# Pair products for one layer of a recommendation tower: four selected features per row instead of one per product tile, and another way of pacing the gathers

## The chip, the core and the metric

The kernel runs on one core of a Trainium2 chip. The metric is the device time of one launch in microseconds (us). A profiled execution gives the span (first to last instruction), and the engines are named as the profile does: PE (TensorE, with PEld for its weight loads), DVE (VectorE), ACT (ScalarE), POOL (GpSimd), SP (SyncE, which issues the ordinary DMAs).

## The reference

512 rows of input each carry 39 ids. Each id picks 16 numbers from its own table, so a row becomes 39 features of 16 numbers (`D`). Then:

```python
# X0, Xi: [b, 39, 16]
z  = einsum('bmd,bnd->bdmn', X0, X0)      # all products of two features
Xi = einsum('bdp,po->bod', z, W0)         # layer 1: 39*39 products -> 128
z  = einsum('bmd,bnd->bdmn', X0, Xi)      # 39 features by 128 outputs
X2 = einsum('bdp,po->bod', z, W1)         # layer 2 -> 128
h  = concat([sum over d of Xi, sum over d of X2, dense_ctx])
y  = relu(relu(h @ W_top1 + b1) @ W_top2 + b2) @ W_top3
```

The product of features n and m is the same as that of m and n, so layer 1 needs 39*40/2 = 780 products, with the two weights added.

## The kernel before

**Tiles, chunks, steps.** The 512 rows are 4 tiles of 128 (`TILES`). A tile is 4 chunks of 32 rows; a chunk is 32*16 = 512 columns (`CH`). Products are laid out over partitions: 780 of them are 7 product tiles (`PT`), six of 128 partitions and a last one with the remaining few, which stand there three times (for a high, a low and a second high part). One product tile of one chunk is one step `s`; 16 chunks times 7 are 112 steps (`STEPS`), 28 a tile (`SPT`). All engines run through the same list of steps in order, each with its own part of the work, and meet at semaphores.

**A step.** PE selects one factor for each of the 128 partitions with a matmul against a 0/1 matrix (`select`, 117 rows, because each feature is held as three bf16 parts) into one of two PSUM banks `b_bank`. DVE multiplies it by the other factor (`multiply`). That other factor, `xa`, is selected once a chunk (`fill_a`) and copied to SBUF by ACT (`take_a`). ACT rounds the product to the matmul's reduced type (`round_z`), DVE subtracts to get the remainder (`rest_z`), and PE, 5 steps later (`LAG`), adds weight times product into `l1_bank` in three matmuls: high by high, high by low, low by high (`layer1`). `l1_used` counts these steps. In tile 0 two product tiles of each seven are "direct": the product goes unrounded into one fp32 matmul, with no rounding and no remainder. `selected`, `product`, `rounded` and `remainder` are the semaphores between these parts.

**The rest of a chunk.** When its 7 steps are through, ACT copies the layer-1 result (`take_xi`, L545, at step 7i+11 of chunk i), PE turns it (`turn_xi`), and both it and the turned `xa` (`turn_a`) are split into high and low parts. SP spreads the latter into a block-diagonal matrix `diag` with 8 DMAs a chunk, and `g_block` multiplies the two in 4 blocks. ACT copies each block (`take_g`). `layer2` of a whole tile follows over the next tile's steps, 78 instructions a tile, from step 45 (`S2_AT`). After the last step come the last tile's layer 2 and the end of the top network.

**The features of a tile.** Those of small tables come from a matrix lookup at the start. Those of large tables come from POOL: one indirect DMA (a gather, L355) per table and tile, 98 in all: 20 for tile 0, 20 for tile 1, 29 for tile 2, 29 for tile 3, in this order. From tile 1 on, a fill of a scratch tile and a wait on it stand before each gather. In three groups of columns, features are then split into bf16 parts by ACT and DVE (`keep_top`, `rest_hi` and so on) at steps `SPLIT_AT` of the tile before; they wait for the gathers of their group (`gathered`). PE turns the parts at `X_AT` and ACT copies them into `xs`.

```python
nc.gpsimd.memset(pad[:], 0.0).then_inc(rested, 1)      # POOL, L353
pool.wait_ge(rested, fills_done)
nc.gpsimd.indirect_dma_start(feat[...], None, tables[order[n]], ...)
```

Of the kernel before, what the change touches and what calls it, by code (L numbers as in the profile page):

```python
# [16 lines left out]

# [15 lines left out]
PT = -(-PAIRS // P)  # L33
REST = PAIRS - (PT - 1) * P
REST_AT = (0, F, 2 * F)
REST_LO = 64
REST_ROWS = 96
ROWS = [P] * (PT - 1) + [REST_ROWS]
assert REST <= F and REST_AT[1] >= 32 and REST_AT[1] + REST <= REST_LO <= REST_AT[2] and REST_AT[2] + REST <= REST_ROWS
# [11 lines left out]
DIRECT = [[1, 4], [], [], []]  # L51
WHOLE = 2
Z_LAG = 2
Z_RING = Z_LAG + 2
LEAD = 1
RING = LAG + 2
LOOK_P = 125
# [8 lines left out]
REST_COLS = 192  # L66
FREE_FIRST = 8
W1_PIECES = 3
# [27 lines left out]
def direct(s):  # L96

    return s % PT in DIRECT[s // (CPT * PT)]


SPLITS = [sum(not direct(q) for q in range(s)) for s in range(STEPS)]
DIRECT_STEPS = [s for s in range(STEPS) if direct(s)]
# [8 lines left out]
def build(nc, ids, row_numbers, small_tables, tables, order, dense_t, w0_pair, w0_mirror, w1,  # L111
# [30 lines left out]
    with ctx:  # L142
# [19 lines left out]
        xa = sb("xa", [P, 2, P, D])  # L162
        sel = sb("sel", [R, PT + 1, P], bf16)
        id16 = sb("id16", [P, P], bf16)
        id32 = sb("id32", [P, P])
        z = sb("z", [P, Z_RING, CH])
# [6 lines left out]
        w0_rest = sb("w0_rest", [REST_ROWS, O], f32r)  # L173
# [49 lines left out]
        for (lo, hi), c in zip(classes, class_blocks):  # L223
# [50 lines left out]
        rested = sem("rested")  # L274
# [5 lines left out]
        chunk0_taken = sem("chunk0_taken")  # L280
        xt_hi_done = sem("xt_hi_done")
# [48 lines left out]

        def after(sems, *job):

            k, n = fill[job]
            return sems[k], n + 1
# [5 lines left out]
        def _(pool):  # L340

            pool.wait_ge(ids_in, 16)
            sent, fills_done = 0, 0
# [65 lines left out]
        def _(act):  # L409
# [111 lines left out]
            def round_z(s):  # L521
                rows = ROWS[s % PT]
                if direct(s):
                    return
# [290 lines left out]
        def _(pe):  # L815
# [286 lines left out]
            mlp3(1)  # L1102


def _pairs():

# [93 lines left out]
```

## Time and profile before

| | us |
|---|---|
| median of 3 runs (263.24 to 263.35) | 263.35 |
| the profiled execution's own time | 262.94 |
| its span | 260.9 |
| PE busy | 235.9 (90%) |
| DVE busy | 196.1 (75%) |
| ACT busy | 168.6 (65%) |
| POOL busy | 128.8 (49%) |

Busy time is a union over the instructions of an engine. The ends of matmuls are modelled, so a stretch in which PE is busy throughout means that it was never seen idle, not that every column of its array worked. Starts of instructions on PE are of more use than durations.

### The profile page before, as it was taken

How to read it: one execution, taken by the hardware profiler on the slowest of the kernel's cores; microseconds unless marked ns; L12 is line 12 of the kernel's file. 1: busy time of each engine (PE TensorE's matmuls, PEld its weight loads, DVE VectorE, ACT ScalarE, POOL GpSimd, SP SyncE). 2: the span in 40 equal slices, each digit the busy share in tenths (PEclk: the TensorE clock that was granted, in tenths of full speed). 3: DMA queues.
4: the chain of work that ended last, by engine and by line, in shares of the span. 5: the costliest groups of instructions: out<-in, count | busy, mean ns of one | idle time of the engine just before them, and what ended most of it. 6: DMA issues, size and time to landing. Idle time of an engine off the chain costs nothing.

```text
span 260.9 us, 5243 instructions
## 1 busy us (share of the span) xinstructions
PE 235.9 (90%) x1848; PEld 182.4 (70%) x1848; DVE 196.1 (75%) x341; ACT 168.6 (65%) x324; POOL 128.8 (49%) x180
## 2 busy tenths in 40 slices
PE   4998856989799978939999999999999999999996
PEld 4997733555466754737777777777787888898795
DVE  1799969998879999556889999879989877624001
ACT  4997555675787886547759878686757655466203
POOL 4788888888888888878888882000000000000000
PEclk9999755899999999988999999999999999999999
DMA  5920001545026540200221111010110101010000
GB/s 160 233 45 10 9 5 13 112 83 129 8 27 147 122 96 7 28 8 9 45 33 20 24 11 28 5 25 7 21 16 12 25 1 25 4 25 0 3 0 0
DMA packets 30883, 10.30 MB, mean 39 GB/s; under 512 B 21018, under 2 KB 30138, under 8 KB 30858
## 3 DMA queue, kind: packets, MB, share of 16 engines
q1 hardware_dynamic: 27722, 9.17, 16.3%
q0 software_dynamic: 3136, 0.81, 3.5%
q8 instruction: 14, 0.23, 0.4%
q14 instruction: 11, 0.09, 0.1%
HBM read 7.34 MB, written 0.00 MB: 28 GB/s over the span
## 4 chain that ended last, share of the span: by engine, by line
PE 48%; POOL 26%; DVE 12%; issue 9%; ACT 3%; DMA 2%; DVEq 0%; ACTq 0%
POOL feat L355 21%; PE s_bank L964 11%; POOL pad L353 5%; PE b_bank L904 4%; PE l_bank L925 4%; PE l_bank L927 4%; PE l_bank L926 4%; DVE z L716 3%; DVE w_sb L660 3%; DVE z_lo L730 3%; PE g_bank L949 2%; PE g_bank L950 2%; PE g_bank L951 2%; PE xi_bank L934 1%; ACT g L448 1%
## 5 line engine op out<-in xcount | busy, mean ns | idle before, releaser
L355 POOL DMA_INDIRECT feat<-tbl,ids_sb x98 | 107.3, 1095 | 29.4 <-POOL pad L353 21.1
L716 DVE TENSOR_TENSOR z<-xa,b_bank 128x512 f32<-128x512 f32 (+1 forms) x112 | 76.1, 684 | 17.3 <-PE b_bank L904 13.8
L529 ACT ACTIVATE z_hi<-z 128x512 fp32r<-128x512 f32 (+1 forms) x104 | 65.6, 630 | 18.9 <-DVE z L716 17.5
L730 DVE TENSOR_TENSOR z_lo<-z,z_hi 128x512 fp32r<-128x512 f32 x88 | 60.3, 686 | 0.0
L904 PE MATMUL b_bank<-xs,sel 117*128 117x512 bf16 (+1 forms) x112 | 45.2, 406 | 8.7 <-DVE z L716 8.6
L964 PE MATMUL s_bank<-g,w_sb 128*128 128x128 f32 x312 | 46.3, 278 | 0.0
L964 PEld LDWEIGHTS s_bank<-g,w_sb 128*128 128x128 f32 x312 | 42.2, 192 | 1.3 <-issue 0.7
L925 PE MATMUL l_bank<-z_hi,w_hi 128*128 128x512 f32 x88 | 41.8, 474 | 0.0
L904 PEld LDWEIGHTS b_bank<-xs,sel 117*128 117x128 bf16 (+1 forms) x112 | 11.5, 103 | 38.3 <-DVE z L716 20.7
L537 ACT ACTIVATE g<-g_bank 128x320 f32<-128x320 f32 x64 | 27.7, 432 | 16.3 <-PE g_bank L951 16.0
L927 PE MATMUL l_bank<-z_hi,w_lo 128*128 128x512 f32 x88 | 35.1, 399 | 0.0
L926 PE MATMUL l_bank<-z_lo,w_hi 128*128 128x512 f32 x88 | 35.0, 398 | 0.0
L949 PE MATMUL g_bank<-diag,xit_hi 128*128 128x320 f32 x64 | 29.5, 462 | 3.2 <-ACT g L537 3.2
L353 POOL MEMSET pad<- 128x192 f32 x78 | 21.3, 273 | 0.1
L950 PE MATMUL g_bank<-diag,xit_hi 128*128 128x320 f32 x64 | 20.1, 313 | 0.0
L951 PE MATMUL g_bank<-diag,xit_lo 128*128 128x320 f32 x64 | 19.9, 310 | 0.0
L927 PEld LDWEIGHTS l_bank<-z_hi,w_lo 128*128 128x128 f32 x88 | 16.8, 191 | 3.8
L949 PEld LDWEIGHTS g_bank<-diag,xit_hi 128*128 128x128 f32 x64 | 12.6, 197 | 8.1 <-issue 5.9
L925 PEld LDWEIGHTS l_bank<-z_hi,w_hi 128*128 128x128 f32 x88 | 17.1, 194 | 1.3 <-issue 0.8
L926 PEld LDWEIGHTS l_bank<-z_lo,w_hi 128*128 128x128 f32 x88 | 17.1, 194 | 0.2
L545 ACT ACTIVATE xi<-l_bank 128x512 f32<-128x512 f32 x16 | 9.6, 597 | 9.0 <-PE l_bank L922 9.0
L560 ACT ACTIVATE g<-b_bank,bt_sb 128x384 f32<-128x384 f32 (+1 forms) x8 | 3.7, 473 | 15.8 <-PE b_bank L1005 11.0
(190 smaller groups left out, 368.2 us busy)
## 6 DMA issues: line engine op xcount, KB each, us to landing
diag<-xt SPq DMA_DIRECT2D x128, 20.0 KB
w_sb<-w SPq DMA_DIRECT2D x3, 832.0 KB
feat<-tbl,ids_sb POOLq DMA_INDIRECT x98, 2.4
wt_sb<-wt SPq DMA_DIRECT2D x2, 512.0 KB, 4.7
g<-small SPq DMA_DIRECT2D x1, 770.0 KB
g<-small SPq DMA_DIRECT2D x1, 448.0 KB
w0p<-w_pair SPq DMA_DIRECT2D x1, 448.0 KB
w0m<-w_mirror SPq DMA_DIRECT2D x1, 448.0 KB
```

Source lines behind the costliest of these rows:

```text
L353: nc.gpsimd.memset(pad[:], 0.0).then_inc(rested, 1)
L355: nc.gpsimd.indirect_dma_start(feat[:, bt % 2, n * D:(n + 1) * D], None, tables[order[n]], bass.IndirectOffsetOnAxis(ids_sb[:, bt, order[n ...
L529: nc.scalar.activation(z_hi[0:rows, s % RING, :], z[0:rows, at, :], ACT.Copy).then_inc(rounded, 1)
L537: nc.scalar.activation(g[:, bt % 2, :, block * SB:(block + 1) * SB], g_bank[:, 0:SB * GW].rearrange("p (b m) -> p m b", m=GW), ACT.Copy).t ...
L716: nc.vector.tensor_tensor(target, xa[0:rows, bt % 2, c * CB:(c + 1) * CB, :].rearrange("p b d -> p (b d)"), b_bank[s % B_RING][0:rows, :], ...
L730: nc.vector.tensor_sub(low[first:rows, s % RING, :], z[first:rows, SPLITS[s] % Z_RING, :], z_hi[first:rows, s % RING, :].bitcast(f32)).the ...
L904: nc.tensor.matmul(b_bank[s % B_RING][0:ROWS[t], :], sel[:, t, 0:ROWS[t]], columns(bt, c), start=True, stop=True).then_inc(selected, 1)
L925: nc.tensor.matmul(bank[:], w0_hi[:, t, :], z_hi[:, slot, :], start=t == 0, stop=False)
L926: nc.tensor.matmul(bank[:], w0_hi[:, t, :], z_lo[:, slot, :], start=False, stop=False)
L927: nc.tensor.matmul(bank[:], w0_lo[:, t, :], z_hi[:, slot, :], start=False, stop=False).then_inc(l1_used, 1)
L949: nc.tensor.matmul(o, y_hi, x_hi, start=True, stop=False)
L964: last = nc.tensor.matmul(s2_bank[:, 0:P], w1_sb[:, order[m], :], g[:, bt % 2, m, :], start=m == 0, stop=m == F - 1)
```

## The change

It does four things.

- **Selection.** Each partition holds four features, chosen so that the six products of two of them (`PRODUCTS`) fill six product tiles. The first factor is selected as before (`fill_a`). Selections 0, 1 and 3 give the other three, selection 2 gives what the last product tile (`REST_T`) multiplies with the first factor. So a chunk has 4 calls of `select` instead of 7. ACT copies selections 0 and 1 to SBUF (`take_factor`); on chunk 0 DVE copies the second of them. `factors` holds three factors of two chunks.
- **Groups.** `multiply`, `round_z` and `rest_z` go by four groups of a chunk: 2 product tiles, 1 (the last tile, 128 rows now, of which 34 get a remainder), 3 and 1. A group is one instruction. `layer1` keeps its 7 steps and its matmuls. A group's buffers are taken again one chunk later. In tile 0 only the last group is direct (one product tile of seven instead of two).
- **Gathers.** The fills are gone. Each gather from the 31st on waits until one more step of layer 1 is done.
- **Times.** The splits, turns and first selections of tiles 2 and 3 stand some steps later in the list; `split_w0` comes before the copy of `xs` on DVE.

```diff
-REST_ROWS = 96
+FACTORS = 4
+PRODUCTS = ((0, 1), (0, 2), (3, 0), (3, 1), (3, 2), (1, 2))
+REST_LO = slice(64, 98)
+T_OF = (0, 1, REST_T, 2, 3, 4, 5)
+GROUPS = ((0, 2, 0, 0), (2, 1, REST_T, 2), (3, 3, 2, 3), (6, 1, 5, 2))
+REST_AT_STEP = {2: 0, 4: 1, 6: 2, 8: 3}
+SELECTS = 4
-DIRECT = [[1, 4], [], [], []]
+DIRECT_CHUNKS = 4
-Z_RING = Z_LAG + 2
+Z_SLOTS = 6
+PACED_FROM = 30
-SPLIT_AT = [[], [8, 14, 19], [8, 14, 19], [9, 16, 21]]
-X_AT = [[], [21, 22], [21, 22], [23, 24]]
-A_AT = [0, 24, 24, 26]
+SPLIT_AT = [[], [8, 14, 19], [9, 16, 23], [9, 16, 23]]
+X_AT = [[], [21, 22], [25, 26], [25, 26]]
+A_AT = [0, 24, 27, 27]
+SELECT_AT = [-4, -2, -1, 0]
+TILE_SELECT_AT = [None, [-4, -2, -1, 0], [0, 0, 1, 2], [0, 0, 1, 2]]
...
-                        if bt:
-                            fills_done += 1
-                            nc.gpsimd.memset(pad[:], 0.0).then_inc(rested, 1)
-                            pool.wait_ge(rested, fills_done)
+                        if bt and sent >= PACED_FROM:
+                            pool.wait_ge(l1_used, sent - PACED_FROM + 1)
...
+            def take_factor(i, k):
+                act.wait_ge(selected, SELECTS * i + k + 1)
+                if i >= 2:
+                    act.wait_ge(product, NG * (i - 1))
+                nc.scalar.activation(factors[:, i % 2, 1 + k, :], b_bank[k][:], ACT.Copy).then_inc(factor_taken, 1)
...
+            def round_z(i, k):
+                if direct(i, k):
                     return
-                act.wait_ge(product, s + 1)
-                if s >= RING:
-                    act.wait_ge(l1_used, s - RING + 1)
-                nc.scalar.activation(z_hi[0:rows, s % RING, :], z[0:rows, at, :], ACT.Copy).then_inc(rounded, 1)
+                first, count, slot, at = GROUPS[k]
+                act.wait_ge(product, NG * i + k + 1)
+                if i:
+                    act.wait_ge(l1_used, (i - 1) * PT + first + count)
+                nc.scalar.activation(z_hi[:, slot:slot + count, :], z[:, at:at + count, :],
+                                     ACT.Copy).then_inc(rounded, 1)
...
+            def multiply(i, k):
+                if k == 0:
+                    ...
+                    target = z[:, 0:2, :]
+                    one = factors[:, i % 2, 0, :].unsqueeze(1).broadcast_to([P, 2, CH])
+                    other = factors[:, i % 2, 1:3, :]
+                elif k == 1:
+                    ...
+                    target, one, other = z[:, 2, :], factors[:, i % 2, 0, :], b_bank[0][:]
+                elif k == 2:
+                    ...
+                    target = z[:, 3:6, :]
+                    one = factors[:, i % 2, :, :]
+                    other = b_bank[1][:].unsqueeze(1).broadcast_to([P, 3, CH])
                 else:
+                    ...
+                    one, other = factors[:, i % 2, 1, :], factors[:, i % 2, 2, :]
+                nc.vector.tensor_tensor(target, one, other, ALU.mult).then_inc(product, 1)
...
+            def select(i, q):
+                if q == 0:
                     features_there(i)
+                if q < 2:
+                    if i:
+                        pe.wait_ge(product, NG * (i - 1) + 2 + q)
+                else:
+                    pe.wait_ge(*taken_factor(i, q - 2))
+                nc.tensor.matmul(b_bank[q % B_RING][:], sel[:, q, :], columns(*divmod(i, CPT)),
                                  start=True, stop=True).then_inc(selected, 1)
```

## Rows read from the trace of the kernel before

**Rows 1.** The page: 40 equal slices of the span, busy tenths and clock.
```profile
PE   4998856989799978939999999999999999999996
PEclk9999755899999999988999999999999999999999
```

**Rows 2.** Windows between copies of a chunk's layer-1 result, then the tail (busy us, instructions).
```profile
core 0: us, PE busy (x) PEld busy (x) DVE busy (x) ACT busy (x) POOL busy (x), PEclk, DMA share, GB/s
54.10:85.08 30.98, 28.67 (x144) 17.89 (x142) 26.95 (x48) 22.35 (x46) 25.27 (x42) 1.00 0.34 72
85.08:107.46 22.38, 19.53 (x102) 13.57 (x100) 22.08 (x40) 16.76 (x35) 19.12 (x25) 1.00 0.33 70
107.46:137.32 29.86, 25.50 (x154) 19.77 (x152) 20.19 (x36) 17.68 (x34) 24.70 (x40) 0.94 0.15 23
137.32:183.91 46.59, 46.19 (x284) 35.47 (x282) 42.28 (x75) 36.17 (x71) 17.68 (x25) 1.00 0.13 18
183.91:229.98 46.07, 45.87 (x286) 37.20 (x285) 35.95 (x61) 27.27 (x55) 0.00 (x0) 1.00 0.09 14
229.98:260.90 30.92, 28.26 (x199) 25.46 (x197) 5.33 (x10) 11.77 (x26) 0.00 (x0) 1.00 0.03 5
```

**Rows 3.** Timeline of ACT: the copy of chunk 6's layer-1 result.
```profile
126.20 0.59 ACT L545 ACTIVATE xi<-l_bank 128x512 f32<-128x512 f32 x1
```

**Rows 4.** The waits over the whole span: total us, times, longest.
```profile
DVE rest L634 <- DMA feat<-tbl,ids_sb: 6.8, 2, 5.4
ACT parts L475 <- DMA feat<-tbl,ids_sb: 6.7, 3, 4.5
```

**Rows 5.** The chain that ended last, around 111 us: start, us, what.
```profile
111.15 2.36 DMA feat<-tbl,ids_sb
```

**Rows 6.** Groups of instructions by form: count, busy us, mean ns, idle before.
```profile
L716 DVE TENSOR_TENSOR z<-xa,b_bank 128x512 f32<-128x512 f32 x96 | 65.4, 685 | 17.3 <-PE b_bank L904 13.8 <-ACT z_hi L529 2.5 <-ACT xa L423 0.7
...
L529 ACT ACTIVATE z_hi<-z 128x512 fp32r<-128x512 f32 x88 | 55.5, 631 | 17.3 <-DVE z L716 15.9 <-PE l_bank L927 0.5
...
L423 ACT ACTIVATE xa<-turn_bank 128x512 f32<-128x512 f32 x15 | 8.9, 593 | 2.5 <-PE turn_bank L882 2.5
...
L793 DVE TENSOR_TENSOR z_lo<-wt_sb,z_hi 128x1024 fp32r<-128x1024 f32 x1 | 1.2, 1227 | 0.4 <-ACT z_hi L591 0.4
L583 ACT ACTIVATE wt_hi<-wt_sb 128x1024 fp32r<-128x1024 f32 x1 | 1.1, 1062 | 0.0
```

**Rows 7.** Timeline of PE: a selection and the matmul behind it.
```profile
185.29 0.39 PE L904 MATMUL b_bank<-xs,sel 117*128 117x512 bf16 x1
185.52 0.60 PE L934 MATMUL xi_bank<-id,xi 128*128 128x128 f32 x4
```

**Rows 8.** Timeline of POOL: gathers without fills, then the first and last with them.
```profile
5.59 0.94 POOL L355 DMA_INDIRECT feat<-tbl,ids_sb  x1 [0.30 <-issue]
6.84 0.94 POOL L355 DMA_INDIRECT feat<-tbl,ids_sb  x1 [0.30 <-issue]
...
32.89 1.48 POOL L355 DMA_INDIRECT feat<-tbl,ids_sb  x1 [0.27 <-POOL pad L353]
...
157.43 1.10 POOL L355 DMA_INDIRECT feat<-tbl,ids_sb  x1 [0.27 <-POOL pad L353]
```

**Rows 9.** Timeline of DVE and POOL: a gather that meets a subtraction of two SBUF operands.
```profile
47.66 0.69 DVE L730 TENSOR_TENSOR z_lo<-z,z_hi 128x512 fp32r<-128x512 f32 x1
47.73 1.44 POOL L355 DMA_INDIRECT feat<-tbl,ids_sb  x1 [0.27 <-POOL pad L353]
48.28 0.69 DVE L716 TENSOR_TENSOR z<-xa,b_bank 128x512 f32<-128x512 f32 x1
```

**Rows 10.** The same two engines where DVE operations follow one another without a pause.
```profile
17.43 2.68 DVE L660 TENSOR_SCALAR w_sb<-xa,numbers 125x2816 bf16<-125x2816 int16 x3
19.67 1.42 POOL L355 DMA_INDIRECT feat<-tbl,ids_sb  x1 [0.30 <-issue]
20.03 0.95 DVE L660 TENSOR_SCALAR xa<-xa,numbers 125x2816 bf16<-125x2816 int16 x1
```

More of the change, by code:

```diff
@@ L32 @@
 PAIRS = F * (F + 1) // 2
[L33 to L36, printed above, removed]
[L37 to L39 removed]
+PT = 7
+FACTORS = 4
+PRODUCTS = ((0, 1), (0, 2), (3, 0), (3, 1), (3, 2), (1, 2))
+REST_T = PT - 1
+REST_LO = slice(64, 98)
+T_OF = (0, 1, REST_T, 2, 3, 4, 5)
+GROUPS = ((0, 2, 0, 0), (2, 1, REST_T, 2), (3, 3, 2, 3), (6, 1, 5, 2))
+GROUP_AT = {first: k for k, (first, count, slot, at) in enumerate(GROUPS)}
+REST_AT_STEP = {2: 0, 4: 1, 6: 2, 8: 3}
+GROUP_OF = [next(k for k, g in enumerate(GROUPS) if g[0] <= u < g[0] + g[1]) for u in range(PT)]
+NG = len(GROUPS)
+SELECTS = 4
 CH = 512
@@ L93, with direct, select_step @@
 XJ = 2
[L96 to L102, printed above, removed]
+def direct(i, k):
+    return k == NG - 1 and i < DIRECT_CHUNKS
+SPLIT_KEYS = [(i, k) for i in range(CHUNKS) for k in range(NG) if not direct(i, k)]
+SPLITS = {key: n for n, key in enumerate(SPLIT_KEYS)}
+def select_step(i, q):
+    bt, c = divmod(i, CPT)
+    return i * PT + (TILE_SELECT_AT[bt] if bt and c == 0 else SELECT_AT)[q]
+SELECT_STEPS = {}
+for i in range(CHUNKS):
+    for q in range(SELECTS):
+        SELECT_STEPS.setdefault(select_step(i, q), []).append((i, q))
 def chunk_at(s, offset):
@@ L720, in rest_z @@
[L720 to L731 removed]
+            dve.wait_ge(selected, 2)
@@ L916, in layer1 @@
-                if t == 0 and i >= 2:
+                    pe.wait_ge(w0_split, 2)
+                if direct(i, k):
+                    pe.wait_ge(product, NG * i + k + 1)
+                else:
+                    pe.wait_ge(remainder, SPLITS[i, k] + 1)
+                if u == 0 and i >= 2:
                     pe.wait_ge(xi_copied, i - 1)
-                if direct(s):
-                    nc.tensor.matmul(bank[:], w0p[:, t, :], whole[(s - SPLITS[s]) % WHOLE][:],
-                                     start=t == 0, stop=False).then_inc(l1_used, 1)
-                elif t == PT - 1:
-                    nc.tensor.matmul(bank[:], w0_rest[:], z_hi[0:REST_ROWS, slot, :],
+                if direct(i, k):
+                    nc.tensor.matmul(bank[:], w0p[:, t, :], whole[i % WHOLE][:],
@@ L1143, in _selections, with _lines, normal @@
-def _selections(pairs):
-    s = np.zeros((R, PT + 1, P), np.float32)
-    for t in range(PT + 1):
-        for p in range(P):
-            m = pairs[t, p, 1] if t < PT else p % F
-            if m >= 0:
-                s[m::F, t, p] = 1.0
+def _lines():
+    points = [v for v in itertools.product(range(3), repeat=4) if next((x for x in v if x), 0) == 1]
+    number = {v: n for n, v in enumerate(points)}
+    def normal(v):
+        lead = next(x for x in v if x)
+        return tuple(x * lead % 3 for x in v)
+    return sorted({tuple(sorted([number[a], number[b]] + [number[normal(tuple((x + c * y) % 3 for x, y in zip(a, b)))]
+                                                          for c in (1, 2)]))
+                   for a, b in itertools.combinations(points, 2)})
@@ L1151, in _selections @@
+def _selections(factors):
+    s = np.zeros((R, SELECTS + 1, P), np.float32)
+    for q in range(SELECTS + 1):
+        for p in range(P):
+            if factors[q, p] >= 0:
+                s[factors[q, p]::F, q, p] = 1.0
     return s
```

285 lines of the change are left out of this document (162 added, 123 removed).

## The prediction

> **What bounds the kernel now.** The page's slices come first [rows 1]: from about 120 us on, PE is hardly ever seen idle, and before that it has holes. Where they are is seen if the span is cut at the copies of chunk results, one every 7 steps [rows 2]. Six stretches come of it. To 54.1: start and chunk 0. To 85.1: chunks 1 to 3, PE 28.7 of 31.0. To 107.5: chunks 4 and 5, DVE 22.08 of 22.38, so DVE bounds. To 137.3: chunks 6 and 7, nothing full. To 183.9 and to 230.0: four chunks each, PE 46.2 of 46.6 and 45.9 of 46.1, so PE bounds, at 11.65 and 11.5 us a chunk. The last 30.9 us are layer 2 and the top network of the last tile.
>
> In the fourth stretch chunk 6 takes 126.20 - 107.46 = 18.7 us and chunk 7 takes 11.1 [rows 2, 3]. The 7.6 us between them are a wait: DVE stood 6.8 us in all, 5.4 of them at once, for a gather [rows 4], and the chain of waits runs over the gather begun at 111.15 and its landing 2.36 us later [rows 5]. That is tile 2's last. So three things take turns: the gathers until 113.5, DVE beside them, PE afterwards.
>
> **PE.** A selection holds PE for 0.23 us: it starts at 185.29 and what follows at 185.52 [rows 7]. It takes about the same before a `g_block`; I use 0.24. Three fewer a chunk are 0.72 us a chunk where PE bounds. Layer 1 keeps its instructions. In tile 0, three split matmuls take the place of one fp32 matmul a chunk; DVE bounds there, so I cost that at nothing (at most 1 us in all if it did not).
>
> **DVE.** A 512-column product takes 685 ns, 1024 columns take 1227 [rows 6]. So 512 columns are 542 ns and the fixed part 143 to 160; three at once are 1.76 us. In tiles 1 to 3, 14 instructions a chunk become 8, which by durations saves 6 times 0.15, or 0.9 us. But independent ones overlap: 47.66 to 48.28 is 0.62 for a 0.69 us instruction [rows 9]. By starts, 0.61 each, 14 take 8.5, and the 8 (two of 1.23, two of 1.76, four of 0.69, less 0.08 each) take 8.1. The bounds are 0.4 and 0.9; I take 0.5, nearer to the starts, since this stretch runs without pauses. In tile 0, 12 instructions of five and seven tiles become 7 with one tile more: 7.3 to 7.5, a loss of 0.2 a chunk.
>
> **ACT.** Rounding 512 columns is 0.63 us, 1024 are 1.06, so three are 1.49 [rows 6]. Seven roundings (4.4) become four (0.63 + 0.63 + 1.06 + 1.49 = 3.8), and two copies of 0.59 come in: 0.6 us more. ACT was busy 36.17 of 46.59, 9.0 a chunk [rows 2]; 9.6 of about 10.9 still fits. Its cover is only PE's time. If it is late, what comes late next is `take_g`, and with it PE's next `g_block`.
>
> **Order of the queues.** The group of three at step 7i+3 waits for layer 1 at PE's step 7i+3, then takes 1.5 us on ACT. Behind it stands a `take_g` (0.43 us), for which PE's `g_block` waits at step 7i+5, one step (1.6 us) and a selection later: 1.9 against 1.8 us, about even. Its remainder (1.8 us on DVE) is then through about 3.3 us after the release, and PE wants it at step 7i+8, 6 us after. At a tile's start the first selections of tiles 2 and 3 stand in step 0 and go through ACT to DVE, some 2.5 us, while PE still has five steps queued. So I expect small stalls: 0 to 0.85 us a chunk, and take 0.25, for the even race.
>
> **Gathers.** Without a fill they start 1.25 us apart (0.94 and 0.30) [rows 8]. With it, (157.43 - 32.89)/77 = 1.617, which is 0.95 + 0.54 and 0.12 of lengthening. The lengthening has a cause in the rows: the gather at 47.73 meets a subtraction that ends at 48.35 and lasts 1.44 instead of 0.95 [rows 9]. It goes on 0.13 us before DVE is through. It hits where DVE has two SBUF operands under way as the gather begins, so on average it costs the sum of (length - 0.13)²/2 over the chunk's time. Before: seven of 0.69 a chunk are 1.1, and the splits 0.1, over 11 us: 0.11, against 0.12 seen. After: the first and last product, too, read SBUF twice, and the instructions are longer. Two of 1.23 give 2.42, one of 1.76 gives 2.66, three of 0.69 give 0.94; half of 6.0, and the splits, over 10.6 us are 0.30. So a gather takes 0.95 + 0.30 + 0.30 = 1.55 us: most of what the fill gives back is lost again. Tile 1's first starts at 32.89 less the fill's 0.27, or 32.6, and five quick ones with one lengthening bring the 26th to 39.4. Tile 2's last (43 further) starts at 106.0 and lands at 108.4. Tile 3's last (72 further) starts at 151.0 and lands at 153.3. The new waits don't bind after the first few: the last, for 68 steps, is met some 5 us before POOL comes to it, and nothing else is queued on POOL behind it. The bounds of the pitch are 1.25 (no lengthening) and 1.96 (below).
>
> A rule to weigh: the Trainium skill, SBUF — State Buffer, section "Who interferes with whom", says that a `tensor_tensor` takes only the shared port's read interface, and infers that it doesn't hold up the making of descriptors. This trace disagrees, with 0.49 us on the gather at 47.73 [rows 9]. By the page the pitch would be 1.25, the last landing at about 132 us, and the sum below the same, for the gathers are hidden either way.
>
> **The sum**, by the stretches of [rows 2]:
> - to 54.1: DVE's weight split moves into its pause before 37 us (gain 1.2), against 0.6 for the copied factor, longer first products, and a selection that stands ahead of the first layer-1 step and waits for the third product. -0.3 (from -1.5 to +1.5).
> - to 85.1: 3 chunks by +0.2; tile 1's last gather (14 after the 26th) lands at 61.1 + 2.4 = 63.5 instead of 32.9 + 19 x 1.62 + 2.4 = 66.1, so DVE's other wait, 6.8 - 5.4 = 1.4 us [rows 4], goes. -0.8 (-3 to +1.5).
> - to 107.5: two chunks by 0.5 on DVE, and ACT's third wait for a gather: 6.7 - 4.5 - 1.3 = 0.9 us, if one of its other two was that of DVE [rows 4]. -1.9 (-3 to 0).
> - to 137.3: two ordinary chunks, 2 x (11.1 - 0.72 + 0.25) = 21.3 instead of 29.86. -8.6.
> - to 183.9 and 230.0: 4 x (0.25 - 0.72) each. -1.9 and -1.9.
> - the tail: nothing changes. 0.
>
> Together -15.4. The gathers fit: step 51, where tile 2's last is wanted, comes at 104.5 + 5 x 1.5 = 112, after 108.4. Step 79, where tile 3's is wanted, comes 19 steps of 1.6 after 125.7, at 156.0, after 153.3. The profiled execution's own 262.94 (span 260.9 and 2.0 around it) becomes 247.5; the median lies 0.4 above the profile, so 247.9 us.
>
> **Rivals.**
> - *Gathers still bind.* If long instructions catch them more often than at random, the pitch is 1.7: tile 3's last lands at 39.4 + 72 x 1.7 + 2.4 = 164.2, 8.2 after step 79, so about 256 us. It costs nothing up to a pitch of 1.59. For it: the margin is only 2.7 us in 117. Against it: the estimate by lengths gave 0.11 where 0.12 was seen.
> - *Coarse groups starve PE.* ACT and DVE hand over later, and PE loses 0.85 instead of 0.25 us a chunk over 12 chunks: 255 us. For it: the race above; three engines within a tenth of each other. Against it: in tile 3 DVE has 10 and ACT 19 of 46 us free [rows 2].
> - *Better than forecast.* No stalls (-2.5) and DVE's full 0.9 (-0.8), a start that gains 1.2 more: 243.5 or less.
> - *Slower.* A gather held by one DVE instruction is caught by the next that follows without pause. The last product, the remainder of three and the first product stand in a row, 3.7 us; with 3.57²/2 the lengthening is 0.71 and the pitch 1.96. Tile 3's last lands at 182.9, 26.9 late: 275 us. It decides from a pitch of 1.80, at which the whole gain is gone. Against it: at 19.67 a gather lasted 1.42 though DVE went on at 20.03 with no pause, so it slipped in between [rows 10]. Those have one operand.
> - *Nothing changes*, the lengthening and stalls eating just the gain: little room for it.
>
> **How the numbers follow.** Forecast 0.52 (243 to 251), gathers bind 0.18 (251 to 260), PE starved 0.17 (251 to 258), better 0.06, slower 0.05, nothing 0.02. The range from 241.5 to 256 holds the forecast, the better case and about half to two thirds of the two slow ones. A measurement of this kernel tells 0.2% (0.5 us) from no change. Faster 0.93, same 0.02, slower 0.05.
>
> **What would show it.** Selections 64 instead of 112, about 10.9 us between chunk copies from the fifth stretch on, PE idle under 3%. DVE groups of 1.23 and 1.76 us. Gathers of 1.25 us on average, the last tile 3 one starting near 151 us. No wait of DVE on a gather above 1 us. The forecast is wrong if gathers average over 1.3 us, if PE waits for `take_g` or a remainder by more than 0.5 us a chunk, or if PE's clock, which fell with its pauses before 50 us [rows 1], falls in later stretches too.

## The result and the profile after

The changed kernel takes 269.93 us (median of 6, 268.25 to 271.01) against 263.35 (262.86 to 264.29, 6 runs) beside it: a ratio of 1.023, interval 1.019 to 1.028. It is slower by 6.6 us where 15.4 less were forecast; the forecast of 247.9 and its range (241.5 to 256) are both missed. The profiled execution took 270.31 us, its span is 268.5. Some executions of a kernel fall in a slower state with a lower granted clock: ratios here and below leave them out while the medians hold them (so on chips 1 to 3 below the medians do not divide to the ratio), and the profiles of E8 and E9 are of such executions.

The page's slices, to be set against [rows 1]:
```profile
PE   4887854976889969895899798788999999989996
PEclk9999755799799999999999999999999999999999
```
PE has holes right through to some 190 us, where it was full from some 120 on. The same windows as [rows 2], cut at the same copies:
```profile
57.24:89.61 32.37, 27.06 (x132) 17.70 (x132) 27.09 (x33) 24.35 (x46) 23.89 (x22) 0.95 0.31 69
89.61:111.78 22.17, 18.36 (x94) 13.06 (x94) 21.23 (x27) 17.33 (x34) 17.60 (x16) 1.00 0.36 73
111.78:139.20 27.42, 23.20 (x146) 18.08 (x146) 19.09 (x23) 18.35 (x34) 16.14 (x14) 1.00 0.15 23
139.20:190.93 51.73, 44.62 (x270) 34.73 (x270) 41.20 (x51) 38.11 (x69) 16.13 (x13) 1.00 0.11 16
190.93:237.52 46.59, 44.20 (x274) 36.65 (x275) 33.83 (x40) 27.76 (x51) 0.00 (x0) 1.00 0.09 15
237.52:268.50 30.98, 28.24 (x199) 25.42 (x197) 5.33 (x10) 11.67 (x26) 0.00 (x0) 1.00 0.02 4
```
By stretch, forecast and measured: to the first copy -0.3 and +3.1; then -0.8 and +1.4, -1.9 and -0.2, -8.6 and -2.4, -1.9 and +5.1, -1.9 and +0.5, 0 and +0.1. In the fifth stretch PE has less work than before, yet the stretch is 5 us longer: PE is busy 44.62 of 51.73 us. No engine is full there. The waits of the whole span say who waits for whom:
```profile
ACT z_hi L558 <- PE l_bank L982: 17.8, 17, 3.0
...
PE g_bank L1004 <- ACT g L567: 14.9, 19, 1.7
DVE z L772 <- ACT factors L454: 14.4, 5, 6.7
...
PE turn_bank L916 <- ACT parts L510: 6.5, 3, 2.5
```
The kernel before has this row for the same copies:
```profile
PE g_bank L949 <- ACT g L537: 3.2, 5, 1.4
```
Then PE stood 3.2 us for copies of `g`; now it is 14.9, in 19 places. DVE's wait for gathers [rows 4] is in this list no more: that part of the change did its work. DVE waits for copied factors instead.

The durations came out as costed [rows 6]:
```profile
L785 DVE TENSOR_TENSOR z_lo<-z,z_hi 128x1536 fp32r<-128x1536 f32 x16 | 28.1, 1757 | 9.4 <-ACT z_hi L558 8.9
...
L558 ACT ACTIVATE z_hi<-z 128x1536 fp32r<-128x1536 f32 x16 | 23.8, 1485 | 22.5 <-PE l_bank L982 13.3 <-DVE z L772 9.2
```
1.76 and 1.49 us were forecast; the second row shows that most of the idle time ahead of the big rounding is a wait for PE. How an ordinary chunk (number 13) goes:
```profile
200.61 1.49 ACT L558 ACTIVATE z_hi<-z 128x1536 fp32r<-128x1536 f32 x1 [1.03 <-PE l_bank L982]
202.00 0.42 ACT L567 ACTIVATE g<-g_bank 128x320 f32<-128x320 f32 x1
202.47 0.42 PE L1004 MATMUL g_bank<-diag,xit_hi 128*128 128x320 f32 x1 [0.61 <-ACT g L567]
```
ACT stands 1.03 us until layer 1 has given back the three buffers, rounds for 1.49, and only then copies `g`, whose block had been there since 199.4; PE is idle for 0.61 us until that copy is done. PE's layer 1 releases ACT's rounding, and the instruction behind the rounding releases PE. And how tile 2 begins:
```profile
121.23 1.48 ACT L558 ACTIVATE z_hi<-z 128x1536 fp32r<-128x1536 f32 x1 [2.12 <-PE l_bank L982]
122.62 0.41 ACT L510 ACTIVATE parts<-rest 128x128 bf16<-128x128 bf16 x1
...
123.17 0.63 PE L916 MATMUL turn_bank<-id,parts 128*117 128x128 bf16 x8 [2.04 <-ACT parts L510]
...
131.19 1.23 DVE L772 TENSOR_TENSOR z<-factors 128x1024 f32<-128x1024 f32 x1 [6.68 <-ACT factors L454]
```
The last split of the tile (`keep_next`) stands behind the rounding of three, the turn behind it, the selections behind that, and DVE idles 6.68 us.

### The profile page after: what moved, and what is told of

Its sections match the earlier page's. It is cut to its first block, busy times and chain, and to the rows that moved or that the text cites. A ratio compares the mean times of both kernels' runs of the same rounds, so it can differ in the third digit from the quotient of the medians.

```text
span 268.5 us, 4887 instructions
## 1 busy us (share of the span) xinstructions
PE 227.0 (85%) x1804; PEld 177.6 (66%) x1804; DVE 194.0 (72%) x249; ACT 177.0 (66%) x311; POOL 115.8 (43%) x102
## 4 chain that ended last, share of the span: by engine, by line
PE 49%; DVE 19%; issue 15%; ACT 15%; DMA 1%; DVEq 0%; ACTq 0%
PE s_bank L1019 10%; DVE z L772 7%; PE l_bank L982 4%; PE l_bank L980 4%; PE l_bank L981 4%; PE g_bank L1004 4%; DVE w_sb L693 4%; DVE z_lo L785 3%; ACT g L567 3%; PE xi_bank L989 2%; PE b_bank L960 2%; PE g_bank L1005 2%; PE g_bank L1006 2%; ACT parts L510 2%; ACT xs L437 1%
## 5 line engine op out<-in xcount | busy, mean ns | idle before, releaser
L378 POOL DMA_INDIRECT feat<-tbl,ids_sb x98 | 115.6, 1179 | 46.5 <-PE l_bank L982 21.4
L558 ACT ACTIVATE z_hi<-z 128x512 fp32r<-128x512 f32 (+2 forms) x60 | 58.7, 978 | 37.9 <-DVE z L772 19.8
L785 DVE TENSOR_TENSOR z_lo<-z,z_hi 128x1024 fp32r<-128x1024 f32 (+2 forms) x44 | 55.8, 1269 | 9.9 <-ACT z_hi L558 9.4
L772 DVE TENSOR_TENSOR z<-factors 128x1024 f32<-128x1024 f32 (+1 forms) x32 | 30.6, 958 | 15.5 <-ACT factors L454 14.4
L772 DVE TENSOR_TENSOR z<-factors,b_bank 128x512 f32<-128x512 f32 (+1 forms) x32 | 38.9, 1216 | 1.1
L1004 PE MATMUL g_bank<-diag,xit_hi 128*128 128x320 f32 x64 | 25.5, 399 | 15.0 <-ACT g L567 14.9
L960 PE MATMUL b_bank<-xs,sel 117*128 117x512 bf16 x64 | 26.4, 424 | 5.2 <-DVE z L772 4.8
L960 PEld LDWEIGHTS b_bank<-xs,sel 117*128 117x128 bf16 x64 | 6.5, 101 | 24.3 <-issue 14.0
L454 ACT ACTIVATE factors<-b_bank 128x512 f32<-128x512 f32 x31 | 18.4, 600 | 3.7 <-PE b_bank L960 3.6
L982 PEld LDWEIGHTS l_bank<-z_hi,w_lo 128*128 128x128 f32 x92 | 17.8, 193 | 4.0
L1005 PE MATMUL g_bank<-diag,xit_hi 128*128 128x320 f32 x64 | 19.8, 309 | 0.0
L792 DVE TENSOR_TENSOR xit_lo<-xi_bank,xit_hi 128x512 fp32r<-128x512 f32 x16 | 11.0, 686 | 5.4 <-ACT xit_hi L581 5.3
```

What stands on the lines that cost most here:

```text
L378: nc.gpsimd.indirect_dma_start(feat[:, bt % 2, n * D:(n + 1) * D], None, tables[order[n]], bass.IndirectOffsetOnAxis(ids_sb[:, bt, order[n ...
L558: nc.scalar.activation(z_hi[:, slot:slot + count, :], z[:, at:at + count, :], ACT.Copy).then_inc(rounded, 1)
L772: nc.vector.tensor_tensor(target, one, other, ALU.mult).then_inc(product, 1)
L785: nc.vector.tensor_sub(z_lo[:, slot:slot + count, :], z[:, at:at + count, :], z_hi[:, slot:slot + count, :].bitcast(f32)).then_inc(remaind ...
L960: nc.tensor.matmul(b_bank[q % B_RING][:], sel[:, q, :], columns(*divmod(i, CPT)), start=True, stop=True).then_inc(selected, 1)
L982: nc.tensor.matmul(bank[:], w0_lo[:, t, :], z_hi[:, t, :], start=False, stop=u == PT - 1).then_inc(l1_used, 1)
```

## The experiments

The kernels were run in five groups, each beside the kernel before on one chip, and each group on a chip of its own. "Copy 0" is when chunk 0's layer-1 result is copied (54.1 before, 57.2 after); "to the end" runs from there to the end of the span (206.8 before, 211.3 after).

| chip | kernel | us | ratio, interval | copy 0 | to the end |
|---|---|---|---|---|---|
| 1 | before | 275.34 | | | |
| | E1 g copies first | 284.89 | 1.052, 1.038 to 1.066 | 77.0 | 207.3 |
| | E2 early turns | 295.89 | 1.097, 1.087 to 1.106 | 85.0 | 208.1 |
| | E3 fills back | 280.87 | 1.041, 1.032 to 1.050 | 66.1 | 210.3 |
| | E4 before, gathers alone | 282.61 | 1.047, 1.032 to 1.062 | 75.5 | 204.3 |
| 2 | before | 272.58 | | | |
| | E5 = E1 and E2 | 290.71 | 1.078, 1.061 to 1.094 | 85.7 | 202.8 |
| | E6 = E1 again | 283.87 | 1.054, 1.044 to 1.063 | 77.7 | 205.1 |
| | E7 = E4 again | 281.57 | 1.050, 1.037 to 1.063 | 75.1 | 204.5 |
| | E8 the changed kernel | 294.52 | 1.091, 1.076 to 1.106 | 76.9 | 217.0 |
| 3 | before | 274.64 | | | |
| | E9 before, as a run | 271.52 | 0.990, 0.981 to 0.998 | 66.3 | 208.5 |
| | E10 rounding by slot | 302.09 | 1.117, 1.105 to 1.129 | 77.7 | 222.6 |
| | E11 E10, E1 and E2 | 309.73 | 1.142, 1.128 to 1.156 | 88.0 | 220.6 |
| | E12 E10 and E1 | 302.10 | 1.116, 1.110 to 1.122 | 77.8 | 222.1 |
| 4 | before | 264.20 | | | |
| | E13 changed, gathers after lookup | 269.63 | 1.021, 1.016 to 1.026 | 56.6 | 209.7 |
| | E16 E13, g copies first | 259.71 | 0.983, 0.979 to 0.987 | 56.9 | 201.1 |
| | E14 E16 and early turns | 259.08 | 0.983, 0.980 to 0.987 | 57.1 | 199.3 |
| | E15 E4, gathers after lookup | 256.50 | 0.973, 0.969 to 0.976 | 54.9 | 199.6 |
| 5 | before | 264.59 | | | |
| | E17 E14, xs copies first | 252.16 | 0.954, 0.950 to 0.957 | 56.7 | 193.4 |
| | E18 E17 without lookup wait | 252.46 | 0.952, 0.949 to 0.956 | 56.4 | 192.2 |

On chips 1 to 3 every kernel reaches copy 0 late, so there only "to the end" is read for the loop. E8's 217.0 and E9's 208.5 are not used. E9 is the kernel before against itself and gives 0.990, so a ratio of chip 3 is good to about 1%. The changed kernel itself was run beside the others only on chip 2.

### E1, E6, E16: the copies of g ahead of the rounding

```diff
                 for i, q in SELECT_STEPS.get(s, []):
                     if q < 2 and i:
                         take_factor(i, q)
-                if s < STEPS and s % PT in GROUP_AT:
-                    round_z(s // PT, GROUP_AT[s % PT])
-                ...
                 for r, at in enumerate(G_AT):
                     if (i := chunk_at(s, at)) is not None:
                         take_g(SUBS * i + r)
+                if s < STEPS and s % PT in GROUP_AT:
+                    round_z(s // PT, GROUP_AT[s % PT])
```

> The changed kernel, with ACT's copy of a g block put ahead of the rounding in each step. Theory A (ACT's queue: the rounding of three waits for PE's layer 1, and the copy that PE wants next stands behind it): PE's wait for g copies falls from 14.9 us to under 4, and the time from 269.9 to 260 to 264 us. Theory B (the tile starts, where the first selections stand in step 0): that wait falls, but the time moves by under 3 us, and DVE still idles over 6 us at once. Theory C (the gathers without fills are what costs): within 1 us of the changed kernel.

> The same kernel as the run with g copies first, again, for its first run stood on a chip with a long start. Theory A: 207 us or less from chunk 0's copy to the end (207.3 in the first run), 260 to 265 us in all if the start is as short as in the profile of the changed kernel. Theory C: as the changed kernel, 211 us and 269.

> The changed kernel with gathers after the lookup and g copies first, turns as the change has them. Beside the run with all three it gives what the turns are worth: theory B 2 to 5 us slower than it; if the turns are worth nothing, within 1 us.

E1 and E6 take 207.3 and 205.1 us from copy 0 on; in all they are slower than before, with their late starts. The cleanest pair is E13 and E16, one chip and this one edit: 269.63 and 259.71 us, 9.9 less (theory A gave 260 to 264), and the sign against before turns. E13's waits hold the same two rows as the changed kernel's:
```profile
ACT z_hi L560 <- PE l_bank L984: 17.1, 16, 3.0
...
PE g_bank L1006 <- ACT g L569: 14.9, 19, 1.7
```
In E16 both are down, and it is ACT that waits for PE's block of `g`:
```profile
ACT g L569 <- PE g_bank L1008: 16.8, 20, 1.7
...
ACT z_hi L560 <- PE l_bank L984: 2.4, 3, 1.2
...
PE g_bank L1006 <- ACT g L569: 0.7, 2, 0.5
```
The last four chunks before the tail take 42.3 us against 46.6 in E13, but E16's cut flatters it: PE had already run a step of layer 1 and a block of `g` ahead of it, and the cut holds 268 instructions of PE. E14, with the same copies of `g` in front and its early turns ahead of these chunks, has 275 in them:
```profile
184.69:227.02 42.33, 42.32 (x268) 35.59 (x267) 33.66 (x41) 27.17 (x51) 0.00 (x0) 1.00 0.09 14
182.19:225.38 43.19, 43.19 (x275) 36.58 (x274) 33.72 (x40) 27.20 (x52) 0.00 (x0) 1.00 0.09 15
```
The first row is E16's, the second E14's. So the place of the copy is worth 46.6 - 43.2 = 3.4 us in these chunks, 0.85 a chunk. One instruction's place in ACT's queue, with no work added or removed, is worth more than the three selections saved (0.72).

### E10, E12, E11: is it the grain of the rounding?

The rival to the queue's order was that three tiles in one rounding are too coarse. E10 rounds the group of three slot by slot, one a step, each waiting for one buffer:

```diff
+            def round_one(i, j):
+                first, count, slot, at = GROUPS[2]
+                if i:
+                    act.wait_ge(l1_used, (i - 1) * PT + first + j + 1)
+                last = nc.scalar.activation(z_hi[:, slot + j, :], z[:, at + j, :], ACT.Copy)
+                if j == count - 1:
+                    last.then_inc(rounded, 1)
```

> The changed kernel, with ACT's rounding of the group of three as three instructions, one a step, each waiting for its own product tile's layer-1 step of the chunk before (two steps earlier than the last one of the group). Theory A: ACT's wait for PE's layer 1 (17.8 us) goes to under 4, PE's wait for g copies under 5 us, DVE's wait for the rounding shrinks, ordinary chunks take 10.1 to 10.6 us instead of 11.1 to 11.4; from chunk 0's copy to the end 203 to 207 us instead of 211.3 to 217. Rival A2 (only the order in ACT's queue counts, not the wait for PE): two more instructions of fixed cost on ACT, so no gain or 1 to 2 us slower. Theory D (PE, with fewer matmuls and more pauses, gets a lower clock, 0.88 in chunk 2 of the changed kernel, and that is most of the loss): ordinary chunks gain, but those with a clock below 1 stay.

> The changed kernel with rounding by slot and g copies ahead of it, turns where the change has them. Theory A alone: as the run by slot within 1 us, for the queue no longer holds anything. Theory B: the pairs of chunks around tile boundaries stay at 26 to 27 us, 2 to 3 us each above the run with all three edits.

> The changed kernel with rounding by slot, g copies ahead of it, and the early turns of tiles 2 and 3. Theories A and B together: the best of all from chunk 0's copy on, 198 to 202 us, ordinary chunks 10.0, tile boundaries at 24 us for the two chunks around them instead of 27.4. Theory D: above 202 us, with a clock below 0.95 in two or more chunks.

E10's expectation failed. Ordinary chunks took 11.8 to 12.0 us instead of 11.1 to 11.4, and PE's wait did not shrink, in E10's waits:
```profile
DVE z_lo L797 <- ACT z_hi L567: 21.2, 10, 2.8
...
PE g_bank L1016 <- ACT g L577: 15.6, 21, 1.6
```
DVE's remainder of three can start only when the third slot is rounded, now two steps later. E1's edit on top leaves the time where it was (E12, 302.10): PE's wait for `g` falls to 1.1 us, but DVE's for the rounding grows to 28.7. E11, from which 198 to 202 us from copy 0 on were expected, took 220.6, the slowest in time of all. So a finer rounding in front of an uncut remainder is no cure, and E16 shows that none is needed: with the coarse rounding as it is, its place was the fault. Rounding and remainder both cut finer were not tried.

### E2, E5, E14: the turns of tiles 2 and 3 earlier

```diff
-SPLIT_AT = [[], [8, 14, 19], [9, 16, 23], [9, 16, 23]]
-X_AT = [[], [21, 22], [25, 26], [25, 26]]
-A_AT = [0, 24, 27, 27]
-TILE_SELECT_AT = [None, [-4, -2, -1, 0], [0, 0, 1, 2], [0, 0, 1, 2]]
-PACED_FROM = 30
+SPLIT_AT = [[], [8, 14, 19], [8, 14, 19], [8, 14, 19]]
+X_AT = [[], [21, 22], [21, 22], [21, 22]]
+A_AT = [0, 24, 24, 24]
+TILE_SELECT_AT = [None, [-4, -2, -1, 0], [-4, -2, -1, 0], [-4, -2, -1, 0]]
+PACED_FROM = 36
```

> The changed kernel, with splits, turns and first selections of tiles 2 and 3 at the steps that tile 1 has, and the gathers paced 6 steps earlier so that they are there. Theory B (tile starts): DVE's waits for copied factors fall from 14.4 us to under 3, the two chunks of 14.4 us at the tile boundaries fall below 12, and the time is 262 to 265 us. Theory A alone: DVE's wait goes but PE goes on waiting for g copies, and the time falls by under 3 us. Theory C: no change, or a new wait for gathers.

> The changed kernel with both edits: g copies ahead of the rounding, and the splits, turns and first selections of tiles 2 and 3 at tile 1's steps (gathers paced 6 steps earlier). On the first chip the stretches before chunk 0 is copied were longer by 9 to 28 us than in the earlier profiles, whatever the kernel, so times are read from that copy on; the changed kernel takes 211.3 us from there, the kernel before 206.8. If the two causes are separate (A and B both true), both savings add: ordinary chunks at about 10.1 us instead of 11.3, tile boundaries at 11 instead of 14.4, from chunk 0's copy to the end 196 us or less, and about 255 us in all on an undisturbed chip. If they are one cause (the later turn only shows what the copies cost), the second edit adds under 2 us to the first: about 204 us from the copy on, 262 in all.

> The changed kernel with three edits: gathers after the lookup, g copies first, early turns. If theories A, B and E hold and add: chunk 0 at 66 to 70 us, 200 to 203 us from there, 268 to 272 in all on such a chip, a ratio of 0.97 to 1.0 to the kernel before. If the start stays long (F): 280 or more.

E2, whose copies of `g` still stand behind the rounding, takes 208.1 us from copy 0 on, and PE waits 10.7 us for `g` there. E5 takes 202.8, between the 196 that separate causes were expected to give and the 204 of a single one. On chip 4 DVE's 6.7 us wait goes, and the chunk interval at a tile's start falls from 14.4 us in E13 and 14.1 in E16 to 10.1 in E14. But the one ahead of it grows from 11.9 in E16 to 15.6: 25.7 for the two against 26.0; in E14 PE's granted clock is 0.89 in the long one, in E16 1.00. E14's time is E16's within 0.6 us. By this pair alone the tile starts would look worth nothing.

### E17: the copies of xs first as well

In E14's long chunk PE stands for a copy of `xs` that is queued on ACT behind a copy of `g` and a rounding:
```profile
112.92 0.44 ACT L569 ACTIVATE g<-g_bank 128x320 f32<-128x320 f32 x1 [0.82 <-PE g_bank L1008]
113.26 1.05 ACT L560 ACTIVATE z_hi<-z 128x1024 fp32r<-128x1024 f32 x1
...
114.20 1.02 ACT L439 ACTIVATE xs<-turn_bank 117x1024 bf16<-117x1024 bf16 x1
...
115.27 0.55 PE L948 MATMUL turn_bank<-id,factors 40*128 40x40 f32 x4 [1.93 <-ACT xs L439]
```

```diff
+                if bt + 1 < TILES:
+                    for k, at in enumerate(X_AT[bt + 1]):
+                        if v == at:
+                            take_x(bt + 1, k)
                 for r, at in enumerate(G_AT):
                 ...
-                    for k, at in enumerate(X_AT[bt + 1]):
-                        if v == at:
-                            take_x(bt + 1, k)
```

> The changed kernel with the copies of g first, the early turns and the wait for the lookup (0.983 on the last chip), and ACT's two copies of xs at the start of a tile moved ahead of the copies of g as well. In that kernel the chunks in which tiles 2 and 3 are turned took 15.6 us each, against 12.9 in the kernel before with unfilled, paced gathers: PE stood 1.9 us for a copy of xs that was queued on ACT behind a copy of g and a rounding of two, then 0.7 for the copy of the turned xa, and its granted clock fell to 0.89. Theory ACT's order: the 1.9 us wait becomes 1.0 (the copy itself), the two chunks take 14.5 us or less, with the clock back at 1.00 13.5, so the time falls by 2 to 4 us, to 0.97 to 0.975 of before. Rival, the work itself (16 transposes and two copies of 1.02 us cannot be hidden in one chunk, whatever the order): the wait moves to g or to the rounding, these chunks stay at 15 us or more, and the ratio stays within 0.4% of 0.983.

The ratio goes from 0.983 to 0.954 (each against the kernel before on its own chip), some 8 us, more than the 2 to 4 us expected. The three chunks in which a tile is turned go from 12.3, 15.6 and 15.6 us to 10.6, 14.8 and 12.3. Part of that is the granted clock, 0.89 in both long chunks of E14 and 0.88 and 1.00 in E17. The middle one missed the 14.5 expected; E18 has it at 13.6 with a clock of 1.00. The copy now starts as soon as the turn is done:
```profile
111.55 1.02 ACT L439 ACTIVATE xs<-turn_bank 117x1024 bf16<-117x1024 bf16 x1 [1.25 <-PE turn_bank L919]
...
113.00 0.65 PE L949 MATMUL turn_bank<-id,factors 40*128 40x40 f32 x4
```
It is the same fault as in the changed kernel, a short copy for PE behind a rounding, in another place. The copies of `xs` first without the early turns were not run, so the two edits are not priced apart.

### E3, E4, E7, E15: the two halves of the change apart

E3 is the changed kernel with the fill and its wait ahead of each gather from tile 1 on, and no pacing; E4 and E7 are the kernel before with the gather part alone:

```diff
                         if bt:
-                            fills_done += 1
-                            nc.gpsimd.memset(pad[:], 0.0).then_inc(rested, 1)
-                            pool.wait_ge(rested, fills_done)
+                        if bt and sent >= 30:
+                            pool.wait_ge(l1_used, sent - 30 + 1)
```

> The changed kernel, with the fill and its wait back before each gather and without the wait for layer-1 steps. Theory C (the gathers are what costs): 262 to 265 us. Theories A and B: the gathers were hidden, so 269 to 274 us, slower only if a pitch of about 0.95 + 0.54 + 0.25 = 1.74 us a gather now ends them after tile 3's last split step (39.4 + 72 x 1.74 = 165 us against 161.6 in the changed kernel).

> The kernel before, with only the gather part of the change: no fills, and from the 31st gather on a wait for one more layer-1 step each. Theories A and B (the loss lies in selection and grouping, the gather part gains what was forecast): the one wait of 5.4 us at 113 us goes, and the time is 254 to 258 us. Theory C: 263 us or more.

> The kernel before with the gather part alone, again for the same reason. If the gather part gains what was forecast: 254 to 258 us with an undisturbed start, chunk 6 at 11 to 12 us instead of 18.7. Theory C: 263 us or more.

> The kernel before with the gather part of the change and tile 1's gathers after the lookup. Theory E: chunk 0 at 64 to 68 us, 204 us from there as in the two runs of the gather part alone, ratio 0.97 to 0.995. F: 281 us again.

Putting the fills back leaves the loop where it was (210.3 us against 211.3 in the changed kernel and 209.7 in E13; the changed kernel's chunk 2 ran at a clock of 0.88 and took 1.6 us more than the same chunk at 1.00), so the gathers' pitch is not what makes it slow. E4 and E7, the gather part alone, take 204.3 and 204.5 us from copy 0 on against 206.8. On chip 4 the gather part (E15) takes 7.7 us off the kernel before: chunks 6 and 7 take 24.0 us instead of 29.9 (chunk 6 12.9, not the 11 to 12 expected), and no wait of DVE for a gather is left. Against E15, the regrouping as made costs 13.1 us (E13) and with its queue mended 3.2 (E16); with the `xs` copies first as well (E17) it gains: 0.954 against 0.973, some 5 us.

### E8, E9, E13, E18: the start

On both chips where profiles with and without fills can be set side by side (chips 1 and 3), the kernels without fills lost 9 to 22 us more ahead of copy 0; on chip 2 they were as late. E8 and E9 are the two kernels unchanged; E13 to E17 hold tile 1's gathers until the lookup is through; E18 is E17 without that wait:

```diff
+                if bt == 1:
+                    pool.wait_ge(looked_up, first_match[-1])
```

> The changed kernel itself beside the others on one chip: 1.023 times the kernel before, 211 us from chunk 0's copy to the end. If its ratio is under 1.01 here, the loss is one of the chip's start and not of the chunks.

> The kernel before, unchanged, as a control with a profile of its own beside the others. From chunk 0's copy to the end it should take 206.8 us as in its first profile, whatever its start takes. If that stretch is longer here by several us, and PE's granted clock lower in it, then the stretches of the other runs must be read against this one.

> The changed kernel, with tile 1's gathers waiting on POOL until the table lookup on PE is through. On these chips PE waited for its own instructions (issue) during the lookup for 15 us in the changed kernel and 3.7 us in the kernel before; all kernels without fills copied chunk 0 at 75 to 88 us, both with fills at 66. Theory E (gathers without fills hold up PE's instruction supply during the lookup): those waits fall under 4 us, chunk 0 is copied at 66 to 70 us instead of 77, and the time falls by 8 us or more against the changed kernel here (294.5). Rival F (it is the chip or the program's place in memory): no change, chunk 0 at 75 us or later.

> The same kernel without the wait that holds tile 1's gathers until the lookup is through: PE's lookup and the gathers run at the same time. Theory: gathers without gaps beside the lookup slow PE's supply of instructions, so chunk 0's copy comes 10 us or more later than in the other run of this call (87 instead of some 57 us), PE shows pauses put down to issue of over 10 us between 10 and 60 us, and the time is 3 to 5% longer. Rival, the chip: the late starts of the first three calls belonged to their chips, not to the gathers; then both runs of this call copy chunk 0 within 1 us of each other and their times differ by under 0.5%. If the chip is one on which neither shows it, the stretch is left open for such chips.

PE's waits between 10 and 60 us in E1, on chip 1:
```profile
PE s_bank L895 <- issue: 5.4, 12, 0.5
PE g_bank L895 <- issue: 4.6, 6, 1.1
PE l_bank L895 <- issue: 3.0, 5, 1.2
PE b_bank L895 <- issue: 2.5, 5, 1.1
```
That is 15.5 us in which PE waited for nothing that the profile shows, in the lookup. The three kernels that let six more gathers go unpaced (E2, E5, E11, with `PACED_FROM` at 36) have the most of it, 19 to 24 us, and the latest copy 0, 85 to 88. E3, the same chip with fills, has 4 us. On chip 5, E18 runs gathers beside the lookup just so and has this:
```profile
PE turn_bank L881 <- issue: 0.5, 1, 0.5
```
E17 and E18 copy chunk 0 at 56.7 and 56.4 us and differ by 0.3 us in time. So the wait bought nothing on that chip, where nothing was late. Of the lateness, some 12 us come with the chip alone (the kernel before, with its fills, has copy 0 at 66.3 instead of 54.1), and the rest needs both, gathers without gaps and such a chip (75 to 88 there, 57.2 and 56.4 elsewhere). Whether the wait would help on such a chip was not tried: E13 and E15, which were to show it, ran on a chip where the kernel before took its usual 264.2 us.

## Why the prediction was wrong

**What held.** The bound by stretches (in E18 PE is busy 43.70 of 44.65 and 43.18 of 43.18 us in the two that it was to bind); the durations; gathers: 1.18 us each on average against 1.25 forecast, tile 2's last begun at 107.14 (106.0 forecast), and DVE's wait for it gone. Tile 3's last began at 161.59 instead of 151, and nobody waited for it; here the statement that the new waits don't bind after the first few failed, for POOL stood 21.4 us in 25 places for layer 1, which was late. In E18, whose chunks take what was forecast and whose waits are six steps looser, the gathers of tiles 2 and 3 take 1.23 us on average and start 1.55 apart, just the forecast pitch, and tile 3's last begins at 149.85. The saving in selections: E18's last four chunks before the tail take 43.2 us against 46.07 before, 0.72 a chunk, just three selections of 0.24. That is E18 cut as [rows 2] are:
```profile
56.38:84.87 28.49, 27.30 (x139) 18.70 (x139) 26.60 (x32) 24.08 (x46) 23.01 (x19) 0.96 0.37 78
84.87:106.12 21.25, 18.64 (x98) 13.36 (x96) 20.30 (x26) 17.20 (x34) 16.98 (x15) 1.00 0.36 75
106.12:129.77 23.65, 21.65 (x141) 17.06 (x140) 19.59 (x23) 18.04 (x34) 18.78 (x17) 1.00 0.18 26
129.77:174.42 44.65, 43.70 (x272) 34.72 (x271) 40.69 (x50) 37.22 (x69) 17.06 (x14) 1.00 0.14 19
174.42:217.60 43.18, 43.18 (x275) 36.59 (x274) 33.73 (x40) 27.17 (x52) 0.00 (x0) 1.00 0.09 15
```
From copy 0 to the end the forecast was 206.8 - 15.1 = 191.7 us; E18 takes 192.2. So near a hit is in part luck: by stretch E18 lies 1.7 below, 0.8 and 2.4 above, level, 1.0 below and 0.1 above the forecast. Still, the sum was that of a kernel whose ACT queue is ordered as E18's, not of the one that was changed. E18's ratio is 0.952 where the forecast's is 0.941; most of the remaining 3 us lie ahead of copy 0.

**The step that failed** is "Order of the queues". It named the right race, the `take_g` behind the rounding of three, and priced it at "about even", 0.25 us a chunk. In the last four chunks, 46.59 us against 46.07 although 2.88 of selections are gone, the loss is 0.85 a chunk, the upper bound given, and E14 gets just that back; over the whole kernel the order costs 9.9 us (E13 against E16). The comparison was 1.9 us of ACT against 1.8 of PE from the release on. In chunk 13's rows ACT takes 1.86 us from the release to the end of the copy (200.61 to 202.47), as forecast, but PE is ready for its `g_block` after 1.25, 0.61 before. And the comparison left out that the race feeds itself: ACT stands until PE's layer 1 has released the buffers (17.8 us in all, 0.5 before), PE then stands for `g`, and so the next release is late too. With this the rival "Coarse groups starve PE" had the right price for these four chunks, not for the whole (255 us); and its name misses the cause, for with the same coarse groups and the copy in front PE waits 0.7 us for `g` in all (E16).

**The same step, at a tile's start.** "While PE still has five steps queued" counted only the way from selection to product. The splits and turns moved with it, and the whole chain of split, turn, copy, selection and product hangs behind the same rounding, and DVE idles 6.7 us instead of being covered. The fifth stretch, forecast at 44.7, took 51.7; of the 7.0, ACT's order for `g` gives back 3.2 (48.5 in E16), and the early turns with `xs` first the rest (44.65 in E18). The early turns without the copies of `xs` in front bring it only to 47.9 (E14).

**The gather wait of 7.6 us** did go, but chunks 6 and 7 took 13.0 and 14.4 instead of 10.65 each, for the two reasons above. Once they are mended, DVE waits for gathers again, in E18:
```profile
DVE rest L668 <- DMA feat<-tbl,ids_sb: 2.7, 2, 2.0
```
That is part of why this stretch takes 23.7 there and not 21.3.

**The start** was put at -0.3 and came to +3.1. DVE's first product starts at 40.14, 0.65 later. The 0.6 for the copied factor came as costed, the gain of 1.2 from the weight split did not: DVE stands 1.62 us for the selection that it copies at 39.36. Most of the rest is ACT's order once more: layer 1 of chunk 0 is through by 54.6, but its copy stands behind the rounding of chunk 1's three:
```profile
55.85 1.49 ACT L558 ACTIVATE z_hi<-z 128x1536 fp32r<-128x1536 f32 x1 [1.05 <-DVE z L772]
...
57.24 0.58 ACT L575 ACTIVATE xi<-l_bank 128x512 f32<-128x512 f32 x1
```
No run moved this copy; that it would give the 2 us back is argued, not shown.

**The rule weighed.** Of the two readings of how a gather meets DVE, the trace bears out the rows' again. A gather that begins at 66.92, under a subtraction of 1.76 us from 66.62, lasts until 69.20: it makes its way from 0.13 us before the subtraction's end (68.38) and then takes its usual 0.95. So does the one at 57.79:
```profile
57.37 1.76 DVE L785 TENSOR_TENSOR z_lo<-z,z_hi 128x1536 fp32r<-128x1536 f32 x1
...
57.79 2.16 POOL L378 DMA_INDIRECT feat<-tbl,ids_sb  x1 [0.30 <-issue]
...
59.05 1.22 DVE L772 TENSOR_TENSOR z<-factors 128x1024 f32<-128x1024 f32 x1
...
66.62 1.76 DVE L785 TENSOR_TENSOR z_lo<-z,z_hi 128x1536 fp32r<-128x1536 f32 x1
66.92 2.28 POOL L378 DMA_INDIRECT feat<-tbl,ids_sb  x1 [0.30 <-issue]
...
107.14 1.27 POOL L378 DMA_INDIRECT feat<-tbl,ids_sb  x1 [0.30 <-PE l_bank L982]
...
161.59 0.94 POOL L378 DMA_INDIRECT feat<-tbl,ids_sb  x1 [0.30 <-PE l_bank L982]
```
The Trainium skill, SBUF — State Buffer, section "Who interferes with whom", infers that a `tensor_tensor` does not hold up the making of descriptors; this case shows it 1.34 us late. Some forty gathers of this trace end by the same sum within 0.02 us. The condition of two SBUF operands holds too: 18 gathers that began under an instruction with one operand in PSUM took 0.94 to 1.04 us. The rival "Slower", by which a gather held once is caught again by the next instruction, did not happen: the gather at 57.79 ends at 59.95 (59.13 - 0.13 + 0.95) although the first product of the next chunk, two SBUF operands, began at 59.05. The mean lengthening is 0.24 us (1.18 against 0.94), against 0.30 forecast, and 0.29 in tiles 2 and 3 of E18. The kernel did come out slower, to which the prediction gave 0.05, but its reason for that case was the gathers, so the chance was not earned by its mechanism.

## What to carry to other kernels

When operations are made coarser, go through every in-order queue and write down what now stands behind the long instruction and which engine waits for that; if the long instruction itself waits for that same engine, it is no even race but a loop, and the short copy belongs in front. A change that is slower can hold a good one: mend the queue before judging the idea, and mend all places that have the same fault, since one of them alone may show nothing (E14). Run the halves of a change apart: here one half gained 7.7 us, the other lost 13.1, and the sum alone showed neither.

## What the runs showed of the hardware

**The same chunk, two clocks.** The window of chunk 2 in the changed kernel, and the second in it with the clock low:
```profile
66.81:80.67 13.86, 11.84 (x61) 8.05 (x62) 9.50 (x11) 10.39 (x19) 10.11 (x9) 0.88 0.11 15
...
69.00:70.00 1.00, 1.00 (x6) 1.00 (x5) 0.77 (x1) 0.24 (x1) 0.69 (x2) 0.50 0.04 5
```
and in E13, with the same instructions on PE in the same order:
```profile
66.19:78.45 12.26, 10.24 (x61) 7.14 (x62) 9.41 (x11) 10.28 (x20) 9.72 (x9) 1.00 0.13 16
```
1.6 us apart, with PE's granted clock at 0.88 of 2.4 GHz on average in the one. In both, PE stood 1.45 us for a copy of `g` just before. In the changed kernel the clock was at 0.50 (1.2 GHz) from about 67.8 to 71.2 us after that, in E13 it stayed at 1.00. So a pause of PE can cost a second time, by the clock, and doesn't each time: E17 and E18 show chunk 6 at 14.81 us with 0.88 and at 13.58 with 1.00. Such a chunk is not to be read from one execution.

**PE short of instructions.** On three of the chips, PE showed 13 to 24 us of pauses put down to issue while gathers without gaps ran beside its lookup (15.5 in E1, 23.7 in E5), 4 us with fills between them (E3), and 0.5 on another chip (E18). What is short then, these runs don't say.
